# A block product moved between the two halves of a convolution, in the later token groups of an AdaLN/FFN kernel

## The reference, cut to what matters

```
x = x + ffn0(cond0(x))     # cond0: grouped convolution, 4 groups, 9 taps, plus a bias per batch and channel
                           # ffn0:  y = c @ W.T + bias + LoRA adapter chosen by batch
x = x + ffn1(cond1(x))     # cond1: 64x64 mix of channels, weights mixed from 8 by attention per batch
                           # ffn1:  16 of 64 rank-16 experts by softmax gates; out = 2 * ((c @ A) * G) @ B
```

## Time and profile before

| | us |
|---|---|
| median of three runs | 649.92 |
| the profiled execution, its own time | 649.55 |
| its span (first to last instruction) | 647.7 |
| TensorE busy (share of the span) | 642.2 (99%) |
| VectorE busy | 448.2 (69%) |
| ScalarE busy | 214.2 (33%) |
| GpSimd busy | 113.0 (17%) |

### The profile page before, as it was taken

One profiled execution on the slowest core, in us unless ns is written; L12 is line 12 of the kernel. 1 busy time (PEld: TensorE's weight loads), 2 busy tenths in 40 slices (PEclk: granted clock), 3 DMA queues, 4 the chain that ended last, 5 costly groups with the idle time before them and its releaser, 6 DMA issues.

```text
span 647.7 us, 8392 instructions
## 1 busy us (share of the span) xinstructions
PE 642.2 (99%) x3176; PEld 533.4 (82%) x3176; DVE 448.2 (69%) x695; ACT 214.2 (33%) x278; POOL 113.0 (17%) x143
## 2 busy tenths in 40 slices
PE   9999999999999999999999999999999999999997
PEld 8878888888897888888889788888889888888885
DVE  2858469549278888558769848636967857666585
ACT  2714135325134124335115312324423421334420
POOL 1499760000000220430000121070000020000000
PEclk9999999999999999999999999999999999999999
DMA  8587844984988976776975794386797676037595
GB/s 301 212 301 268 322 134 148 354 264 173 397 282 326 397 250 274 275 224 242 369 281 205 290 374 169 109 223 248 285 337 262 265 250 261 3 125 235 183 348 218
DMA packets 54570, 164.94 MB, mean 255 GB/s; under 512 B 6756, under 2 KB 7652, under 8 KB 54544
## 3 DMA queue, kind: packets, MB, share of 16 engines
q1 hardware_dynamic: 46240, 148.05, 62.9%
q10 hardware_dynamic: 5328, 9.61, 4.6%
q0 software_dynamic: 2976, 6.95, 3.4%
HBM read 138.23 MB, written 26.36 MB: 254 GB/s over the span
## 4 chain that ended last, share of the span: by engine, by line
PE 96%; DVE 2%; DMA 1%; SPq 0%; ACT 0%; issue 0%; DVEq 0%
PE bank L1513 26%; PE bank L1515 26%; PE bank L1514 26%; PE bank L1527 9%; PE bank L1558 3%; PE bank L1534 2%; PE bank L1564 1%; PE bank L1565 1%; PE bank L1546 1%; DMA gate<-hidden_w 1%; DVE u_lo L1143 1%; DVE work L1063 1%; DVE v_lo L1020 1%; PE bank L1550 0%; PE bank L1552 0%; PE bank L1581 0%
## 5 line engine op out<-in xcount | busy, mean ns | idle before, releaser
L1014 DVE TENSOR_TENSOR piece_lo<-raw,piece_hi 128x1024 fp32r<-128x1024 f32 x60 | 73.5, 1229 | 87.7 <-ACT piece_hi L752 87.7
L1513 PE MATMUL bank<-piece_hi,u_hi 128*128 128x512 f32 x272 | 107.9, 397 | 0.1
L1515 PE MATMUL bank<-piece_hi,u_lo 128*128 128x512 f32 x272 | 107.4, 395 | 0.0
L1514 PE MATMUL bank<-piece_lo,u_hi 128*128 128x512 f32 x272 | 107.3, 395 | 0.0
L752 ACT ACTIVATE piece_hi<-raw 128x1024 fp32r<-128x1024 f32 x60 | 63.3, 1058 | 131.7 <-PE bank L1515 86.8
L1513 PE MATMUL bank<-v_hi,piece_hi 128*128 128x512 f32 x256 | 101.7, 397 | 0.0
L1515 PE MATMUL bank<-v_hi,piece_lo 128*128 128x512 f32 x256 | 101.2, 395 | 0.0
L1514 PE MATMUL bank<-v_lo,piece_hi 128*128 128x512 f32 x256 | 101.1, 395 | 0.0
L1513 PE MATMUL bank<-piece_hi,v_hi 128*128 128x512 f32 x192 | 75.9, 395 | 0.0
L1514 PE MATMUL bank<-piece_lo,v_hi 128*128 128x512 f32 x192 | 75.8, 395 | 0.0
L1515 PE MATMUL bank<-piece_hi,v_lo 128*128 128x512 f32 x192 | 75.8, 395 | 0.0
(11 more groups left out here) (178 smaller groups left out, 823.4 us busy)
## 6 DMA issues: line engine op xcount, KB each, us to landing
raw<-pieces SPq DMA_DIRECT2D x76, 512.0 KB, 5.6
piece_hi<-kept SPq DMA_DIRECT2D x48, 512.0 KB, 5.0
piece_lo<-kept SPq DMA_DIRECT2D x48, 512.0 KB, 6.1
x<-x SPq DMA_DIRECT2D x16, 512.0 KB, 5.4
gate_x<-gates ACTq DMA_DIRECT2D x32, 256.0 KB
out<-x SPq DMA_DIRECT2D x32, 256.0 KB, 4.5
conv_in<-conv_x SPq DMA_DIRECT2D x15, 516.0 KB, 7.1
conv_in<-pieces SPq DMA_DIRECT2D x12, 512.0 KB, 9.5
```

The lines of the kernel that those rows point to most:

```text
L1014: dve.tensor_tensor(piece_lo[:, n % SLOTS, :], raw[:, r % RAWS, :], piece_hi[:, n % SLOTS, :].bitcast(F32), ALU.subtract).then_inc(s_piece ...
L1513: pe.matmul(to, left_hi, right_hi, start=first, stop=False)
L1514: pe.matmul(to, left_hi, right_lo, start=False, stop=False)
L1515: return pe.matmul(to, left_lo, right_hi, start=False, stop=last)
```

## The change

In the later groups, TensorE issues the first product after conv 3 instead of after conv 7, with the same two waits ahead of it (low parts of batches 0 to 3; the group before has added what it read from the banks). VectorE issues lo 3 ahead of item 4 instead of behind it. Nothing is added to or removed from the work, and group 0 is as it was.

```diff
@@ VectorE, group(g) @@
                 for b in range(GB):
+                    if b == GB // 2:
+                        conv_lo(g, b - 1)
                     dve.wait_ge(s_conv, g * GB + b + 1)
                     conv_item(b, CONV_BANKS[b])
-                    if b:
+                    if b and b != GB // 2:
                         conv_lo(g, b - 1)
                     if b == 1:
                         split_raw(g, 3)
@@ TensorE, group(g) @@
                 for b in range(GB):
+                    if b == GB // 2:
+                        split_done(g, CONV0 + 3)
+                        pe.wait_ge(s_o, g * 22 - 6)
+                        winograd(0, (4, 5), u_hi, u_lo, block_of(0, 0), True)
                     if b % 2 == 0:
                         pe.wait_ge(s_convin[b // 2], g * 16 + 16)
                     if b == 0:
...
                         mm = conv(b, CONV_BANKS[b], cg)
                     mm.then_inc(s_conv, 1)
 
-                split_done(g, CONV0 + 3)
-                pe.wait_ge(s_o, g * 22 - 6)
-                winograd(0, (4, 5), u_hi, u_lo, block_of(0, 0), True)
                 pe.wait_ge(s_item, g * ITEMS + CONV0 + 8)
                 winograd(2, (6, 7), u_hi, u_lo, block_of(0, 1), False)
```

## The result

| | before | after |
|---|---|---|
| median us (runs) | 650.09 (4; 649.11 to 651.76) | 676.46 (4; 674.48 to 677.75) |
| ratio, 95% interval | 1 | 1.0399 (1.0378 to 1.042) |
| the profiled execution, own time | 649.55 | 677.75 |
| its span | 647.7 | 675.9 |

What follows compares the result with a forecast made beforehand. TensorE's own stream, busy 99%, bounds the kernel. Waits of 17.65 and 3.03 us plus 0.3 for switches (21.0) and 4.7 of clock add 25.7 us to 649.55: 675.2, or 675.6 as median; range 669.5 to 681.5.

Steps and rivals of the forecast that it cites:

- That nothing can be won: TensorE's stream is the time; its three waits, 1.4 us together, bound what a reordering can win.
- The long waits: TensorE waits for lo 3 ahead of each later group's first product: 6.11, 6.22 and 5.32 us, together 17.65.
- Item 3 starts at the time of before: On VectorE nothing ahead of item 3 changes, so lo 3 ends 2.07 us after item 3's unchanged start.
- The second wait: The second product waits for item 7 after conv 7: 1.01 us in each of three groups, 3.03 us.
- the forecast's own T: Time at which TensorE's next matmul could start after conv 7; the last record ends at T + 0.24.
- The switch: One extra switch from convolution to product a group on TensorE: 0.09 us each, 0.3 us in all.
- The clock: The granted clock falls in the long holes, slowing the first product: 1.6 us a group, 4.7 us in all.
- a stretch at half clock as long as the one for which it held: Basis of the clock term: the clock held 3.2 us at the kernel's end, half of that gives 1.6 us a group.
- Waits alone: Rival: the clock holds through the waits or comes back at once, 670.9 us; chance 22%.
- the clock low throughout: Rival: the product after each wait runs at half pace to its end, 687.6 us; chance 7%.
- A late third product: Rival: the first sum's 0.76 us slack is used up, costing 0.2 to 1.3 us a group, 676 to 680; chance 6%.
- Not slower: Rival: lo 3 ends before conv 3 does, so the wait vanishes, at best 648.5 us; chance 3%.

Runs made afterwards that it cites:

- e9: Changed kernel with e3, e4 and e7 together, plus SyncE's fetch of kept piece 11 moved ahead of raw piece 15: 651.25 us, ratio 1.0012 to before.
- e3: Changed kernel with the first product and its waits after conv 5 instead of after conv 3: 659.8 us, ratio 1.0129 to before.
- e6: Changed kernel with the split of weight piece 3 moved behind lo 3 on VectorE, likewise on ScalarE: 668.8 us, ratio 1.0286 to before.
- e7: Changed kernel with the splits of weight pieces 2 and 3 both moved behind lo 3: 664.13 us, ratio 1.0214 to before.
- e5: Changed kernel with one convolution of batch 0 repeated into bank 1 before the first product's wait: 675.79 us, ratio 1.039 to before.
- e4: Changed kernel with conv 6 and 7 writing banks 0 and 1, so the second product waits for items 0 to 3 only: 676.56 us, ratio 1.0397.
- e11: e7 with one convolution of batch 0 repeated into bank 1 in each wait after conv 3: 661.3 us, ratio 1.0168 to before.
- e2: Changed kernel with the convolution of batch 0 done twice more into bank 1 before the first product's wait: 673.45 us, ratio 1.0355 to before.
- e10: e4 with one transfer of SyncE also moved, the same line as in e9: 675.98 us, ratio 1.0392 to before.

## Why the prediction was right

The mechanism was read right, and the sum came out at 25.7 us against 26.4 between the medians. That it is so close is in part luck: between the two profiled executions, where the terms can be read, it was 28.2 us, and there the long waits were 1.9 us shorter than forecast, the clock's loss 3.1 us longer, and 1.2 us stood in no term.

- *That nothing can be won.* Right as far as e9 shows it, which has every wait of the change covered but 0.6 us, with the first product after conv 5, and is no faster than before.
- *The long waits,* 6.11, 6.22 and 5.32 us forecast; 6.60, 4.63 and 4.56 measured. Mechanism right (e3, e6, e7). "Item 3 starts at the time of before" failed in groups 2 and 3, where it came 9.5 and 9.4 us behind the convolution's start instead of 11.2 and 10.3. What stands ahead of item 0 waits for a raw weight piece, and its transfer took from issue to ScalarE's start 4.0 us in group 2 of after, 5.5 before (339.46 to 343.45, 328.33 to 333.87). Other runs put the lag back: 13.5 us behind the start in e5's group 2. This wait varies by 2 us from run to run; one trace gave it to 0.01.
- *The second wait,* 1.01 us a group: 1.02 measured from the slot of the next record; from the forecast's own T, 0.24 us ahead of the last record's end, it is 0.86 + 0.24 = 1.10. Without it (e4) the first sum was late by 0.24 us, so the slack behind it, read at 0.76 us, was right too.
- *The switch,* 0.09 us a group, small beside 0.3 us a group of changes that I didn't forecast.
- *VectorE idle between lo 3 and item 4* for 7.7 us: 10.5, since the product ran at half clock.
- *The clock,* the mis-sized term: 4.7 us forecast, 7.8 measured (2.62, 2.43, 2.77), above the 2.1 us a group that I took from the kernel's start. That the clock falls was right and is shown by e11. What made it too small is the step "a stretch at half clock as long as the one for which it held": it held for 5.3, 3.0 and 3.7 us of the three holes and was then down for 6.8 us each time, and TensorE was at work in 5.7, 5.3 and 6.1 of them. Each microsecond of work at half clock cost 0.46 (matmuls 0.427 us apart instead of 0.2325), which gives the 7.8 us. The start of the kernel, where I read the 2.1 us, ran at half pace too, although the clock column shows no drop: the trace's clock record begins only 5.25 us behind the span's start (the column prints 1.00 where there is no record), and the starts of TensorE's matmuls are 0.213 us apart up to there and 0.112 behind it. The remark that shorter waits may miss the drop was wrong at the size that I meant (all nine holes from 4.41 us on had it). The Trainium skill ("TensorE: Matmul & The Clock Gate", its table "Why this matters for your kernels") advises against idle gaps of over some 3 us. The holes of after, over 4 us, agree; those of e3, e6 and e7 from 2.3 us on, already expensive, don't.
- *The rivals.* Waits alone (670.9) is refuted: three products at half clock. So is the clock low throughout: it came back within each product. A late third product needs e4's order. Not slower: it needed a VectorE 5.3 us earlier, and item 3 came at most 1.7 us earlier than before.

## What to carry to other kernels

A product that "needs only half" of its operand isn't ready when TensorE has made that half, but when the slowest engine behind TensorE has split it: take the distance from that engine's rows, its backlog from the stage before included, before work is moved forward. On a stream that is 99% busy, a new order can win at most the stream's own waits (1.4 us here), and a hole is paid once as a wait and, in every trace here from 2.3 us on, a second time as slow matmuls behind it. If a hole can't be avoided, work that nobody needs in it can be cheaper than standing still (e11).

## What the runs showed of the hardware that was not expected

The standstill ahead of the first product, the product's time (24 matmuls) and how much of it lay at half clock, group by group, from the timelines and the clock of one trace of each kernel:

| kernel | standstill us | product us | at half clock us |
|---|---|---|---|
| e11 | 0.56, 0.55, 0.55 | 5.67, 5.67, 5.69 | 0 |
| e2, groups 2, 3 | 1.00, 1.02 | 5.67, 5.70 | 0 |
| e3, group 1 | 2.10 | 5.67 | 0 |
| e7 | 2.34, 2.34, 2.34 | 7.23, 7.23, 7.23 | 3.4, 3.4, 3.4 |
| e6, group 3 | 2.44 | 7.23 | 3.4 |
| e3, groups 2, 3 | 2.63, 2.60 | 7.09, 7.07 | 3.1, 3.1 |
| e5 | 2.87, 4.38, 4.38 | 7.26, 7.23, 7.14 | 3.4, 3.4, 3.2 |
| e6, groups 1, 2 | 3.41, 3.84 | 7.25, 7.23 | 3.4, 3.4 |
| e2, group 1 | 3.50 | 7.02 | 3.0 |
| after | 6.45, 4.47, 4.41 | 8.29, 8.10, 8.44 | 5.7, 5.3, 6.1 |
| e4 | 5.70, 4.51, 6.17 | 7.82, 7.76, 7.00 | 4.8, 4.6, 3.0 |
| e10 | 6.14, 6.09, 5.95 | 7.38, 7.22, 7.59 | 3.8, 3.4, 4.2 |

All six standstills up to 2.10 us were free, all 21 from 2.34 us on cost 1.3 to 2.8 us of slow matmuls, and the cost doesn't grow with the standstill's length. It goes with the last column: every product lost 0.45 to 0.47 us for each microsecond that it ran at half clock. The border between 2.10 and 2.34 us is that of these traces and no sharp one, as e7's other executions show. When the clock falls isn't given by the length either. In e7 it fell 0.8 to 1.3 us after TensorE had taken up work again, and in e6 and in groups 1 and 2 of e5 (holes of 2.4 to 4.4 us) between the moment of resuming and 1.3 us behind it; in group 3 of e5, in e3 and in e2 (2.6 to 4.4 us) it fell 0.2 to 0.4 us before the product started, and in after, e4 and e10 0.7 to 3.9 us before. The end of the trace of before, where no work follows, couldn't show that it can fall behind the hole.
